# RWKV attention and mixture of experts on one core: the first batch's token mixes shared out anew between ScalarE, VectorE and GpSimd

## The reference, cut to what matters

```
shifted = x moved by one token
key   = x*mk + shifted*(1-mk)      value, rec: the same with mv, mr      ("token mixes")
k, v, r = key @ Wk, value @ Wv, sigmoid(rec @ Wr)
num, den, out = scan over the tokens, per channel (weights exp of k and of a decay)
x = layernorm(x + (r * out) @ Wo)
x = layernorm(x + top-2-of-8 mixture of experts(x))
```

## Time and profile before

| | |
|---|---|
| median of 3 runs | 459.14 us |
| the profiled execution | 459.16 us, span in the profile 457.4 us |
| TensorE busy | 444.7 us, 97% of the span |
| VectorE, ScalarE, GpSimd busy | 403.4 us (88%), 356.0 us (78%), 312.6 us (68%) |
| TensorE's granted clock over the span | 0.998 of full speed |

### The profile page before, as it was taken

One profiled execution on the slowest core, in us unless ns is written; L12 is line 12 of the kernel. 1 busy time (PEld: TensorE's weight loads), 2 busy tenths in 40 slices (PEclk: granted clock), 3 DMA queues, 4 the chain that ended last, 5 costly groups with the idle time before them and its releaser, 6 DMA issues.

```text
span 457.4 us, 6679 instructions
## 1 busy us (share of the span) xinstructions
PE 444.7 (97%) x1984; PEld 340.2 (74%) x1984; DVE 403.4 (88%) x615; ACT 356.0 (78%) x798; POOL 312.6 (68%) x300
## 2 busy tenths in 40 slices
PE   8999999999999999999999999999999999999993
PEld 3444557777888888888888888888888888888761
DVE  5989989899788989999898998989898996975985
ACT  1666757877788779888788887888798887768685
POOL 2355677588658998579858697569965695653335
PEclk9999999999999999999999999999999999999999
DMA  8703230033000042001420042100520022300016
GB/s 238 225 0 119 92 92 1 1 115 93 1 1 0 2 161 92 24 0 57 142 81 0 1 138 94 47 0 24 162 83 11 1 70 94 138 1 0 0 49 229
DMA packets 20244, 30.64 MB, mean 67 GB/s; under 512 B 2032, under 2 KB 7152, under 8 KB 20208
## 3 DMA queue, kind: packets, MB, share of 16 engines
q1 hardware_dynamic: 20064, 29.95, 20.6%
q10 hardware_dynamic: 144, 0.26, 0.2%
HBM read 21.82 MB, written 8.39 MB: 66 GB/s over the span
## 4 chain that ended last, share of the span: by engine, by line
PE 78%; DVE 4%; ACT 2%; POOL 2%; issue 1%; ACTq 0%; DVEq 0%
PE PH L451 5%; PE PV L332 5%; PE PV L338 5%; PE PR L338 5%; PE PV L333 5%; PE PR L332 5%; PE PK L332 5%; PE PK L338 5%; PE PR L333 5%; PE PK L333 5%; PE PP L361 5%; PE PP L362 4%; PE PP L366 4%; PE PT L433 3%; PE PP L381 2%
## 5 line engine op out<-in xcount | busy, mean ns | idle before, releaser
L594 ACT ACTIVATE PR<-PR 128x512 f32<-128x512 f32 x128 | 74.5, 582 | 29.7 <-PE PR L338 10.5
L1231 POOL TENSOR_TENSOR DQ<-DEN,EX 128x512 f32<-128x512 f32 x32 | 41.4, 1292 | 20.5 <-DVE DEN L890 20.5
L1237 POOL TENSOR_SCALAR NM<-SUM,RS 128x1 f32<-128x1 f32 x30 | 8.0, 268 | 62.0 <-ACT RS L594 62.0
L332 PE MATMUL PK<-KH,WKH 128*128 128x512 f32 x112 | 46.2, 413 | 0.6 <-DVE NUM L907 0.6
L944 DVE SCALAR_TENSOR_TENSOR KT<-D,VEC,XT 128x512 f32<-128x512 f32 x57 | 45.9, 853 | 0.0
L332 PE MATMUL PV<-VH,WVH 128*128 128x512 f32 x112 | 45.6, 407 | 0.0
L338 PE MATMUL PR<-RL,WRH 128*128 128x512 f32 x112 | 44.1, 394 | 0.7 <-POOL RL L1199 0.7
L332 PE MATMUL PR<-RH,WRH 128*128 128x512 f32 x112 | 44.6, 398 | 0.2 <-DVE RW L931 0.2
L338 PE MATMUL PV<-VL,WVH 128*128 128x512 f32 x112 | 43.9, 392 | 0.0
L338 PE MATMUL PK<-KL,WKH 128*128 128x512 f32 x112 | 43.9, 392 | 0.0
L333 PE MATMUL PK<-KH,WKL 128*128 128x512 f32 x112 | 43.8, 391 | 0.0
(11 more groups left out here) (281 smaller groups left out, 1285.5 us busy)
## 6 DMA issues: line engine op xcount, KB each, us to landing
XT<-in_xt SPq DMA_DIRECT2D x32, 256.0 KB, 3.5
XN<-in_x SPq DMA_DIRECT2D x28, 256.0 KB, 2.6
out<-XN SPq DMA_DIRECT2D x28, 256.0 KB, 2.0
X1T<-in_wo SPq DMA_DIRECT2D x1, 1024.0 KB, 5.3
XT<-in_x SPq DMA_DIRECT2D x4, 256.0 KB, 3.2
out<-XT SPq DMA_DIRECT2D x3, 256.0 KB, 2.3
X1T<-in_wk SPq DMA_DIRECT2D x2, 256.0 KB, 4.8
XN<-in_wv SPq DMA_DIRECT2D x2, 256.0 KB, 5.6
```

The lines of the kernel that those rows point to most:

```text
L332: eng.matmul(dst[:, :], wh[:, c, o], high[:, c, :], start=(c == 0), stop=False)
L594: eng.activation(*a, **k).then_inc(q[s], 1)
L1231: eng.tensor_tensor(DQ[:, :], DEN[:, 0:T], EX[:, 1, :], ALU.add).then_inc(q["e"], 1)
```

## The change

- `VEC` is loaded from ScalarE's queue, ahead of its table load, and no longer first on SyncE's.
- Batch 0's key mixes no longer use D. VectorE makes 1 - mk (`OMK`), ScalarE writes `shifted * (1 - mk)` into the mix's buffer (semaphore `y`), VectorE adds `x * mk` in one instruction (`first_mix`).
- All four differences of batch 0 are GpSimd's. Value mixes stay on VectorE; they wait for `d` alone.
- Batch 0's receptance mixes: ScalarE writes `D * mr` (semaphore `rm`), GpSimd adds `shifted` (semaphore `r0`).
- VectorE's order: `scan_max(1)` and `lead(1)` stand before slot 0's scans and no longer behind its `numerator`.
- WKL is made by GpSimd, in four blocks of 128 columns, two in slot 0 and two in slot 1.
- The last of the four matmuls at the start has half the columns.
- Semaphore numbers of `kt` are counted anew (`mixed`), since receptance mixes of batch 0 no longer add to it.

```diff
         @block.sync
             def load_xt(b, c):
-                if b:
-                    eng.wait_ge(q["kt"], 3 * C * (b - 1) + 2 * C + c + 1)
+                if b == 1:
+                    eng.wait_ge(q["kt"], mixed(0, 1, c))
+                    eng.wait_ge(q["r0"], c + 1)
...
-            eng.dma_start(VEC[:, :, :], vec).then_inc(q["vec"], 16)
...
-            eng.wait_ge(q["lwk"], 2)
+            eng.wait_ge(q["lwk"], C)
         @block.tensor
-            for _ in range(4):
-                eng.matmul(PP[:, :], RW[:, 0, 0:128], RW[:, 0, :], start=True, stop=True)
+            for n in (T, T, T, T // 2):
+                eng.matmul(PP[:, 0:n], RW[:, 0, 0:128], RW[:, 0, 0:n], start=True, stop=True)
         @block.scalar
+            eng.dma_start(VEC[:, :, :], vec).then_inc(q["vec"], 16)
             eng.preload_act_table_set(TABLES)
...
+            eng.wait_ge(q["om"], 1)
+            eng.wait_ge(q["cm"], 1)
+            for c in range(C):
+                eng.wait_ge(q[f"xt{c}"], 16)
+                act("y", full(0, 0, c), XT[:, c, 0:T], ACT.Copy, scale=OMK[:, c:c + 1])
+            for c in range(C):
+                eng.wait_ge(q["d"], c + 1)
+                act("rm", full(0, 2, c), D[:, c, :], ACT.Copy, scale=VEC[:, 4, c:c + 1])
             decay_gates(0)
         @block.vector
+            def first_mix(c):
+                eng.wait_ge(q[f"xt{c}"], 16)
+                eng.wait_ge(q["y"], c + 1)
+                eng.scalar_tensor_tensor(out=full(0, 0, c), in0=XT[:, c, 1:T + 1], scalar=VEC[:, 2, c:c + 1],
+                                         in1=full(0, 0, c), op0=ALU.mult, op1=ALU.add).then_inc(q["kt"], 1)
...
+            eng.wait_ge(q["vec"], 16)
+            eng.tensor_scalar(OMK, VEC[:, 2, :], -1.0, 1.0, ALU.mult, ALU.add).then_inc(q["om"], 1)
...
-            difference(1)
-            mixes(0, 0, 0, 1)
-            difference(3)
-            mixes(0, 0, 2, 3)
+            for c in range(C):
+                first_mix(c)
             mixes(0, 1, 0, 1)
             scan_max(0)
             lead(0)
             mixes(0, 1, 2, 3)
-            mixes(0, 2, 0, 1, 2, 3)
+            scan_max(1)
+            lead(1)
...
-                if s < U - 1:
+                if 0 < s < U - 1:
                     scan_max(s + 1)
                     lead(s + 1)
...
-                if s < 2:
-                    low_weights(2 * s)
         @block.gpsimd
-            difference(0, 0)
-            difference(0, 2)
+            for c in range(C):
+                difference(0, c)
+            for c in range(C):
+                eng.wait_ge(q["rm"], c + 1)
+                eng.tensor_tensor(full(0, 2, c), full(0, 2, c), XT[:, c, 0:T], ALU.add).then_inc(q["r0"], 1)
...
+                if s == 0:
+                    low_weights(0, 0, 1)
                 if j == 0 and batch(b + 1):
                     for c in range(C):
                         difference(b + 1, c)
                 if s == 1:
                     low_weights(1, *range(C))
+                    low_weights(0, 2, 3)
```

More of the change, by code:

```diff
@@ L49, in rwkv_moe_postln @@
         VEC = sb("VEC", [128, 5, C])
-        CST = sb("CST", [128, 4, C])
+        CST = sb("CST", [128, 5, C])
         XT = sb("XT", [128, C, T + 1])
@@ L86, in rwkv_moe_postln @@
         UPT = KT[:, 1, :]
-        TD, NTD, CC, QB = (CST[:, i, :] for i in range(4))
+        TD, NTD, CC, QB, OMK = (CST[:, i, :] for i in range(5))
         def full(b, which, c):
@@ L196, in half_at, with mixed @@
             return C - 1 - c if b % 2 else c
+        def mixed(b, which, c):
+            return C * (3 * b + which) + c + 1 - (C if b else 0)
         def halved(t):
@@ L231, in load_xt @@
             def load_xt(b, c):
-                if b:
-                    eng.wait_ge(q["kt"], 3 * C * (b - 1) + 2 * C + c + 1)
+                if b == 1:
+                    eng.wait_ge(q["kt"], mixed(0, 1, c))
+                    eng.wait_ge(q["r0"], c + 1)
+                elif b:
+                    eng.wait_ge(q["kt"], mixed(b - 1, 2, c))
                 eng.dma_start(XT[:, c, 1:T + 1], xt[b, 128 * c:128 * c + 128, :]).then_inc(q[f"xt{c}"], 16)
@@ L237, in load_xn @@
                 if b == LAST:
-                    eng.wait_ge(q["kt"], 3 * C * NB)
+                    eng.wait_ge(q["kt"], mixed(LAST, 2, C - 1))
                     eng.dma_start(XT[:, n, 1:T + 1], x[b, 128 * n:128 * n + 128, :]).then_inc(q[f"xt{n}"], 16)
@@ L316, in whole @@
                     if u == 0:
-                        eng.wait_ge(q["kt"], C * which + c + 1)
+                        eng.wait_ge(q[("kt", "kt", "r0")[which]], c + 1 + (C if which == 1 else 0))
                     last = eng.matmul(dst[:, :], stage[:, c, o], full(0, which, c), start=(c == 0), stop=(c == C - 1))
@@ L327, in split @@
                     eng.wait_ge(q["hw"], which + 1)
-                    eng.wait_ge(q[("lwk", "lwv", "lwr")[which]], j + 1 if which else 2)
+                    eng.wait_ge(q[("lwk", "lwv", "lwr")[which]], j + 1)
                 for c in range(C):
@@ L633, in highs @@
                 for c in chunks:
-                    eng.wait_ge(q["kt"], C * (3 * b + which) + c + 1)
+                    eng.wait_ge(q["kt"], mixed(b, which, c))
                     if b > 1 and c < C - 1:
@@ L933, in mix @@
             def mix(b, which, c):
[L934 to L937, removed]
+                eng.wait_ge(q["d"], C * b + c + 1)
                 if b and which < 2:
@@ L1253, in _ @@
                               pattern=[[-1, 128]], channel_multiplier=1).then_inc(q["idn"], 1)
-            difference(0, 0)
-            difference(0, 2)
+            for c in range(C):
[3 more added lines that the diff above has]
+                eng.tensor_tensor(full(0, 2, c), full(0, 2, c), XT[:, c, 0:T], ALU.add).then_inc(q["r0"], 1)
             def low_weights(i, *blocks):
-                stage, high, low, done = ((XN[0], WVH, WVL, "lwv"), (XN[1], WRH, WRL, "lwr"))[i - 1]
+                stage, high, low, done = ((X1T, WKH, WKL, "lwk"), (XN[0], WVH, WVL, "lwv"), (XN[1], WRH, WRL, "lwr"))[i]
                 eng.wait_ge(q["hw"], i + 1)
```

## The result

The changed kernel takes 463.01 us (median of 4 runs, 462.87 to 463.16) against 459.1 of the kernel before: ratio 1.0084, 95% interval 1.0071 to 1.0097. It is 3.9 us slower, where 0.5 was forecast, and it is outside the range of 457.4 to 460.7. The profiled execution took 463.16 us with a span of 461.4, so 4.0 more span than before.

A forecast was written before the change was run, and what follows sets the result against it. TensorE was taken as the bound, busy from 65.9 us on, so only the start and slots 0 to 3 counted: +1.35 at v's second block, -0.85 taken back, +0.5 on 459.16, giving 459.66 (written 459.6); range 457.4 to 460.7.

The forecast's parts named there:

- The port: Start and WKL: VectorE mixes and GpSimd tensor_tensors work one at a time; per turn mix 0.55, GpSimd difference 0.89 us.
- The turns: Start: mixes alternate with GpSimd's differences, then its receptance sums, putting `scan_max(0)` at 13.0 against 11.30, 1.7 us later.
- rival 1: Start: no turns come about, `scan_max(0)` at 10.4, v's second block at 20.7; time 457.1 to 457.9; chance 0.29.
- the low halves' release: End of slots 0 to 3: GpSimd's last low half of batch 1's receptance ends about 66.3 instead of 65.8.
- The small load itself: Start: the vectors' load, now before ScalarE's table load, is done with 1 - mk well before 3.76; hidden.
- over 1.2 us each: Sign in the new profile: the start's four key mixes take this long, a GpSimd difference inside each wait.
- The 0.6 at the numerator scan: Before 65.9 us: TensorE's 0.6 us wait; with VectorE's part 0.5 shorter it would swallow the rest, sum 0.
- the section on slots 0 to 3: Slots 0 to 3: of 1.35 us lost at v's second block, 0.85 is taken back by v's fourth.
- the meeting of WKL and the three mixes: Slot 1: VectorE's batch 1 mixes wait for the port from 35.65 to 36.8, ending at 38.7.
- Its sum: Whole kernel: +1.35 at v's second block, -0.85 to v's fourth, = +0.5 us on 459.16: 459.66.
- the first part: What bounds the kernel: TensorE, busy 444.7 of 457.4 us, in every stretch from 65.9 up to 400 us.

The follow-up runs named there:

- the kernel of the three edits: Changed kernel on the old places, with GpSimd's receptance sums held, vectors on SyncE's queue and two 32-byte pads: 458.78 us, 0.9993 to the kernel before.
- The vectors' own run: Changed kernel with CST at 8 rows, the VEC load put back at the head of SyncE's queue: 462.57 us against 462.79.

## Why the prediction was wrong

**Right, by its own steps.** The port decides the start. The turns came about at the value mixes (forecast 1.7 each, measured 3.25 / 2 = 1.6) and put `scan_max(0)` at 13.54 (forecast 13.0, rival 1 10.4), `scan_den(0)` at 18.84 (18.55), v's second block at 23.53 (23.24), v's fourth at 44.30 (43.9) without a gap for TensorE between, and the low halves' release at 66.76 (66.3). What is lost at the last is 0.88 for 0.45. Single traces of one order of work spread there with the landings of the inputs, from 65.83 to 66.43 in the nine with the old order and from 66.41 to 67.17 in the five with the changed one and no further edit to it; their medians, 65.88 and 66.59, are 0.71 apart. Rival 1 fell. Holding the sums back took 1.7 us of turns away, so their part is shown, not only argued. On the Trainium skill's page "SBUF — State Buffer" (section "SBUF: two separate sides"), which lets one of the two engines hold the port for a whole instruction: the trace agrees that one waits for the other, but a mix and a sum in turn took 1.6 us where their free times add to 0.74 + 1.27 = 2.0, so a part of each start is hidden, as in the earlier trace rows.

**Wrong in the start.** The vectors were costed at nothing. "The small load itself" was to be there "well before 3.76"; it was used at 3.75, 3.0 us after its issue, where it took 1.6 on SyncE's queue. VectorE's 1 - mk then took 0.92 us instead of 0.17 beside GpSimd's first difference, `y` began at 4.79 and the first mix at 5.87, when the forecast had it ended at 5.35. In this trace that lateness was taken up again, because another term was off by more: the third input chunk. The first difference began at 3.69 (forecast 3.76), but the third only at 7.41 (forecast 6.24 for the landing, 6.67 in the kernel before). VectorE had done two mixes by 7.29 and GpSimd two differences by 5.72, and both then stood idle. So the first three key mixes took 0.75, 0.75 and 0.81 us, not the "over 1.2 us each" that was to show the forecast right, and the turns began only with the third difference. From the landing on the sizes are those of the forecast: the third mix ends at 9.00, the fourth difference at 9.89 (0.89 later), the fourth mix at 10.45 (0.56 later), where 9.67 was forecast. In the kernel of the three edits, with the vectors on SyncE's queue, 1 - mk ran at 2.40 in 0.17 and the fourth mix ended at 9.81, but there the third chunk had landed at 6.64 too. The vectors' own run puts their price at 0.2 us (462.57 against 462.79), which is within the noise.

The Trainium skill's page "DMA: Bandwidth & Descriptors" (section "Issuing engines are not separate DMA queues") promises no more than issue time from another queue. The trace agrees: the first two chunks landed 0.5 and 0.8 us sooner than before, but the third 0.7 and the fourth 0.3 us later, and the small load lost 1.4.

**The 0.6 at the numerator scan** was left as a remark in the section on slots 0 to 3: were VectorE 0.5 shorter, that wait would swallow the rest. With the low blocks later it did so in part: 459.75, the wait 0.26 for 0.61, and 0.5 us over the kernel before are left. The forecast took the meeting of WKL and the three mixes into its times, but did not say that this meeting keeps the lost time from being won back. (Its sum, 459.66, is rounded to 459.6 where it should be 459.7; nothing hangs on that.)

**The step that failed** is in the first part: from 65.9 us on "nothing that this change touches is waited for there, and what is won or lost before 65.9 us is carried to the end". The second half is the one that cost most. A TensorE that waits for nothing has a time of its own, matmuls times pace, and I took the pace as given because neither the clock nor the matmuls changed. The fifth row of CST was costed as one small instruction; its place was not costed at all. It is worth 463.01 - 460.34 = 2.7 us, and 2.8 as an unused row in the kernel before: five times the forecast's whole sum. With it the forecast would have been 462.3. The first half fails too, by less. The claim was read from stretches up to 400 us; at 405.75 (408.49 in the changed kernel) TensorE waits for ScalarE, and this makes 0.35 us of the order's 1.1. So against the sum's 0.5, the order of work cost 0.7 in the start and slots 0 to 3, and 0.35 where nothing was expected.

## What to carry to other kernels

When the bound engine has no gaps, count its instructions and measure the distance between their starts, before and after, ahead of any talk of waits. Read the waits to the end of the span: here one that counted lay at 405.75, behind the last stretch that was read. Ask of every edit which tiles it moves in memory: a row added to a small tile in the middle of the allocations moves all tiles behind it. Put new small tiles last, and try a few pads on a tuned kernel, since they change neither result nor order. And where work goes to GpSimd, lay its instructions beside VectorE's two-input ones: a wait that keeps them apart was worth 1.7 us here (458.78 to 457.12).

## What the runs showed of the hardware that I had not expected

- The pace of 128x512 matmuls depends on the places of tiles: 0.2276 to 0.2335 us at a granted clock of 1.00 throughout, 2.6%. Moving all tiles behind CST by 32, 128, 192, 256 and 512 bytes gave 462.01, 461.77, 458.64, 459.25 and 459.40 us against 459.2 (the 32 and 128 were dear, 256 and 512 free); moving the weights with them by 64 gave 459.16. That fits a period of 256 bytes. Why is open, and so is what the pads ahead of RW and X1T add once the halves lie at 0 modulo 256 (0.2291 to 0.2277). I had no run that moves one of these tiles by itself there.
- A load of 128 rows of 80 bytes, issued from ScalarE's queue at 0.73 us beside SyncE's large ones, was used 3.0 us later; at the head of SyncE's queue it took 1.6. In seven traces with the first order it landed at 3.44 to 3.83 us, in thirteen with the second at 2.30 to 2.54. The third input chunk, issued 0.5 us sooner in the seven, landed at 6.00 to 7.73 us there and at 6.52 to 7.07 in the thirteen: it varied more and came no sooner.
- A VectorE instruction on 128x4 elements with one input took 0.92 us (free 0.17). It began at 3.83 inside GpSimd's difference of 1.04 us from 3.69 and ended with it (4.75 and 4.73): not only the large two-input ones wait. It took 0.90 to 0.92 us in all seven traces in which it met that difference, and 0.17 or 0.18 in the four in which it ran ahead of it.
- A pause of 0.27 us of VectorE, ahead of one scan near 390 us and ended by nothing that the trace shows, is in every trace with the changed order of work and in none with the old one. It cost 0.35 us, at a wait of TensorE 16 us later.
